# First attention of a two-layer kernel: another order of steps, later weighing of masked steps, and part of the second squares on ScalarE

## The reference

```python
# 16 heads of d = 16; rotary and a layernorm per head on q and k
a = einsum('bhnd,bhmd->bhnm', q, k) ** 4
a = tril(a)
out = einsum('bhnm,bhmd->bhnd', a / sum(a, -1), v) @ w_out
```

## Time and profile before

| | |
|---|---|
| three runs | 1670.02, 1672.91, 1682.65 us, median 1672.91 |
| profiled execution | 1666.9 us, of which the span of the trace is 1665.2 us |
| TensorE clock granted, mean | 0.88 of 2.4 GHz |
| TensorE busy | 1369.2 us (82%) |
| VectorE, ScalarE, GpSimd busy | 1083.1, 830.2, 570.2 us (65%, 50%, 34%) |
| first attention, both batches' steps | from 74 to 201 us and from 270 to 434 us |

### The profile page before, as it was taken

How to read it: one execution, slowest core, us unless ns; L and a number is a source line. 1 busy time by engine, 2 the same in 40 slices (tenths; PEclk the granted TensorE clock), 3 DMA queues, 4 the chain that set the end, 5 groups by cost and what they waited for, 6 DMA issues and landing times.

```text
span 1665.2 us, 27032 instructions
## 1 busy us (share of the span) xinstructions
PE 1369.2 (82%) x10104; PEld 880.1 (53%) x10104; DVE 1083.1 (65%) x2291; ACT 830.2 (50%) x1208; POOL 570.2 (34%) x674
## 2 busy tenths in 40 slices
PE   6377755686689999799999899889999886999982
PEld 4233443342468877444444555444554353799971
DVE  7678896866553354867777566667767545455676
ACT  2466625665343343236666355566657531366660
POOL 7477344547201103110111001001110476666660
PEclk8599985987789999759999899989989877999996
DMA  2690000002211100000000000000001355577875
GB/s 88 212 353 35 1 1 1 1 1 86 72 43 64 39 17 27 16 1 1 2 2 1 1 1 1 1 1 1 2 1 64 141 197 197 166 213 211 259 260 205
DMA packets 69078, 124.36 MB, mean 75 GB/s; under 512 B 7319, under 2 KB 55127, under 8 KB 67929
## 3 DMA queue, kind: packets, MB, share of 16 engines
q1 hardware_dynamic: 56664, 85.92, 16.1%
q0 software_dynamic: 12288, 36.72, 5.9%
HBM read 60.22 MB, written 62.39 MB: 74 GB/s over the span
## 4 chain that ended last, share of the span: by engine, by line
PE 56%; DVE 23%; POOL 8%; ACT 7%; issue 4%; DMA 1%; POOLq 0%; SPq 0%; DVEq 0%; ACTq 0%
PE psum L2283 10%; PE psum L2156 9%; PE psum L2256 6%; PE psum L2466 6%; DVE probs L2837 5%; PE psum L2373 4%; PE psum L2216 4%; DVE neg_max L2819 4%; PE psum L2489 3%; PE psum L2233 3%; PE psum L2394 3%; POOL many_x L3430 3%; PE psum L337 2%; POOL probs L3368 2%; ACT probs L2579 2%
## 5 line engine op out<-in xcount | busy, mean ns | idle before, releaser
L2579 ACT ACTIVATE probs<-psum 128x1024 f32<-128x1024 f32 (+1 forms) x480 | 437.4, 945 | 269.4 <-PE psum L2270 140.6
L2819 DVE TENSOR_REDUCE neg_max<-psum 128x1 f32<-128x512 f32 (+3 forms) x768 | 380.0, 551 | 132.5 <-PE psum L2233 118.4
L2256 PE MATMUL psum<-qt,kt 32*128 32x512 f32 (+6 forms) x1152 | 242.8, 454 | 31.0 <-ACT probs L2579 10.3
L2283 PE MATMUL psum<-probs,v 128*32 128x256 f32 (+3 forms) x2048 | 187.2, 453 | 58.4 <-POOL probs L3368 42.8
L2837 DVE TENSOR_TENSOR probs<-probs 128x1024 f32<-128x1024 f32 (+1 forms) x152 | 199.9, 1372 | 45.6 <-ACT probs L2579 45.2
L2216 PE MATMUL psum<-kt,qt 32*128 32x512 f32 (+3 forms) x768 | 205.2, 458 | 19.9 <-DVE neg_max L2819 18.5
L2256 PEld LDWEIGHTS psum<-qt,kt 32*128 32x128 f32 (+1 forms) x1152 | 108.9, 199 | 192.3 <-issue 98.4
L342 POOL TENSOR_SCALAR q_rows<-neg_max 128x16 fp32r<-128x16 f32 x32 | 7.1, 221 | 539.0 <-DVE neg_max L2827 358.8
L3437 POOL DMA_INDIRECT results<-sp_y,sp_row x128 | 124.8, 975 | 64.2 <-ACT sp_y L2634 37.6
L2216 PEld LDWEIGHTS psum<-kt,qt 32*128 32x128 f32 x768 | 96.0, 197 | 46.9 <-DVE neg_max L2819 39.1
L2156 PE MATMUL psum<-ident,q_rows 128*128 128x128 f32 x384 | 67.8, 320 | 57.8 <-ACT k_rows L2508 51.1
(11 more groups left out here) (327 smaller groups left out, 2602.1 us busy)
## 6 DMA issues: line engine op xcount, KB each, us to landing
many_x<-blank SPq DMA_DIRECT2D x2, 10240.0 KB, 50.9
sp_xs<-many_x SPq DMA_DIRECT2D x64, 320.0 KB, 3.7
sp_w<-in_sparse SPq DMA_DIRECT2D x8, 1280.0 KB, 10.2
x_turned<-results SPq DMA_DIRECT2D x8, 768.0 KB, 6.4
sp_back<-results SPq DMA_DIRECT2D x8, 768.0 KB, 9.2
sorted_x<-blank SPq DMA_DIRECT2D x2, 1152.0 KB, 6.5
sorted_y<-y SPq DMA_DIRECT2D x18, 128.0 KB, 1.7
rows<-in_x SPq DMA_DIRECT2D x4, 512.0 KB, 7.0
```

The lines of the kernel that those rows point to most:

```text
L2256: inst = pe.matmul(psum[:, base - early:base + QCH - q0], A.kt[rows, k_slot, key * P:(key + 1) * P], A.qt[rows, q_slot, c * QCH + q0 - ear ...
L2283: inst = pe.matmul(psum[32 * h:32 * h + 32, bank + q0:bank + q1], A.v_of(b)[:, key, col:col + 32], A.probs[:, slot, h, at:at + q1 - q0], s ...
L2579: act.activation(dst, view, ACT.Exp if A.softmax else ACT.Square).then_inc(exped.by(A.layer, b, quad, c, step, h0), 1)
L2819: inst = dve.tensor_reduce(A.neg_max[:, g % 2, 0 if last else 1, tile, h0 + i:h0 + i + 1], bank[:, at * P:(at + cols) * P], X_AXIS, ALU.ma ...
```

## The change

1. The steps of a quad run in the order of `MIXED_STEPS`, those of a batch's first quad in that of `FIRST_STEPS`.
2. A masked step is weighed after three further steps in place of two; unmasked ones after two as before. Which weighing opens and closes a bank is counted (`first`, `closes`) in place of taken from the step's number.
3. The second square of three halves, (1,1) h0=2, (1,2) h0=2 and (1,3) h0=0, is done by ScalarE right behind its first; GpSimd squares none.
4. The second half's cuts and turns of quad 0's groups move from before the quad into it, at places 0 to 2.
5. The next quad's cuts and turns stand at `CUT_PLACES`: cuts of the first group at 2.5 to 4 and its turn at 6 in a first quad, at 0 to 2.5 and 5 otherwise; of the second group at 4.5 to 6.2 and 9, or 4 to 6 and 8. Before: 0 to 2.4 and 3.75, 3.5 to 5.9 and 7.25.
6. Normalizing of the quad before stands at 3 (before 2.5); in the last quad chunk 0 is normalized at 8, turned at 9 and projected at 10, behind the last step (before 5.5, 7, 8.5).

```diff
+FIRST_STEPS = ((0, 0), (0, 1), (0, 2), (1, 0), (1, 4), (1, 1), (1, 5), (1, 2), (1, 6), (1, 3))
+RAISED_ON_ACT = ((1, 1, 2), (1, 2, 2), (1, 3, 0))
+MIXED_STEPS = ((0, 0), (1, 0), (0, 1), (0, 2), (1, 1), (1, 4), (1, 5), (1, 2), (1, 6), (1, 3))
+CUT_PLACES = (((2.5, 3, 3.5, 4, 6), (4.5, 5, 6.1, 6.2, 9)), ((0, 1, 2, 2.5, 5), (4, 4.5, 5.5, 6, 8)))
...
-                    def weigh_due():
-                        while due and len(due) >= WEIGHTS_AHEAD + (A.softmax and due[0][2] == 0):
-                            weigh()
+                    def weigh_due(n):
+                        for entry in [e for e in due if n - e[5] >= WEIGHTS_AHEAD + (e[2] >= 4 * e[1])]:
+                            weigh(entry)
...
-                            on_pool = c == 1 and step == 3 and h0 == 0
-                            if poly:
-                                done = mark(pool_raised if on_pool else raised, L, b, quad, c, step, h0)
+                            on_act = (c, step, h0) in RAISED_ON_ACT
+                            if on_act:
+                                done = mark(exped, L, b, quad, c, step, h0, "raised")
+                            elif poly:
+                                done = mark(raised, L, b, quad, c, step, h0)
...
-                        due.append((quad, c, step, p_slot, tuple(ready)))
-                        if poly and len(due) > WEIGHTS_AHEAD:
-                            weigh()
+                        n = next(steps_done)
+                        due.append((quad, c, step, p_slot, tuple(ready), n))
+                        weigh_due(n)
...
-                    else:
-                        for g in (0, 1):
-                            cut(g, HALF, TILES, hurry=True)
-                            turn(g, HALF, TILES)
...
-                            between.append((2.5, lambda q=quad - 1: normalize(q)))
+                            between.append((3, lambda q=quad - 1: normalize(q)))
+                        else:
+                            for g in (0, 1):
+                                between.append((g, lambda g=g: cut(g, HALF, TILES, hurry=True)))
+                                between.append((1 + g, lambda g=g: turn(g, HALF, TILES)))
...
-                            between.append((5.5, lambda q=quad: half_done.append(normalize(q, 0, HALF))))
-                            between.append((7, lambda: turn_out(0, half_done[0])))
-                            between.append((8.5, lambda: project_out(0)))
+                            between.append((8, lambda q=quad: half_done.append(normalize(q, 0, HALF))))
+                            between.append((9, lambda: turn_out(0, half_done[0])))
+                            between.append((10, lambda: project_out(0)))
...
# ScalarE
             def scores(A, b, quad, c, step, h0, p_slot, p_free, slot, qk_done, on_act, **_):
...
                 act.activation(dst, view, ACT.Exp if A.softmax else ACT.Square
                                ).then_inc(exped.by(A.layer, b, quad, c, step, h0), 1)
+                if on_act:
+                    q.wait_ge(exped, A.layer, b, quad, c, step, h0)
+                    act.activation(dst, dst, ACT.Square
+                                   ).then_inc(exped.by(A.layer, b, quad, c, step, h0, "raised"), 1)
...
# GpSimd
-            def scores(A, b, quad, c, step, h0, p_slot, slot, on_pool, **_):
-                if A.softmax or not on_pool:
-                    return
-                view, dst = scored_view(A, c, step, h0, p_slot, slot)
-                q.wait_ge(exped, A.layer, b, quad, c, step, h0)
-                pool.tensor_tensor(dst, dst, dst, ALU.mult).then_inc(pool_raised.by(A.layer, b, quad, c, step, h0), 1)
-                q.wait_ge(pool_raised, A.layer, b, quad, c, step, h0)
```

More of the change, by code:

```diff
@@ L731, in turn_max, with weigh @@
                            q_free=q_free, before=before)
[L733 to L738, removed]
+                    due, o_turn, chunk_weighed, steps_done = [], {}, {}, count()
+                    def weigh(entry):
+                        quad, c, step, slot, ready, _ = entry
+                        due.remove(entry)
+                        n = chunk_weighed.setdefault((quad, c), 0)
+                        chunk_weighed[quad, c] = n + 1
+                        first, closes, oc, oc_free = n == 0, n == len(key_steps(c)) - 1, None, ()
+                        bank_free = o_free[c] if first else ()
                         done = mark(weighed, L, b, quad, c, step, None)
                         probs_ring.give(slot, done)
-                        closes, oc, oc_free = step == len(key_steps(c)) - 1, None, ()
                         if closes:
@@ L910, in plan_attention @@
                         between.sort(key=lambda p: p[0])
-                        for n, (c, step) in enumerate((c, step) for c in range(SEQ // QCH) for step in range(len(key_steps(c)))):
+                        for n, (c, step) in enumerate(MIXED_STEPS if quad else FIRST_STEPS):
                             half_steps = weights(quad, c, step, beside[2 * n:2 * n + 2])
@@ L918, in plan_attention @@
                             what()
-                    while due:
-                        weigh()
+                    for entry in tuple(due):
+                        weigh(entry)
                     before_next = fence()
@@ L1095, in weigh @@
                     do("weigh", A=A, b=b, quad=quad, c=c, step=step, part=part, slot=slot, waits=(*ready, *bank_free),
-                       closes=closes, oc=oc, oc_free=oc_free)
+                       first=step == 0 and part == 0, closes=closes, oc=oc, oc_free=oc_free)
                 def weigh_due(half):
@@ L2272, in scores, with weigh @@
                     inst.then_inc(scored.by(A.layer, b, quad, c, step, h0), 1)
-            def weigh(A, b, quad, c, step, part, slot, waits, **_):
+            def weigh(A, b, quad, c, step, part, slot, waits, first, closes, **_):
                 bank = A.out_bank(c)
-                steps = key_steps(c)
                 for e in waits:
                     q.wait_ge(*e)
-                whole = [(key, first_query(c, key), QCH, at) for key, at in steps[step][0]]
+                whole = [(key, first_query(c, key), QCH, at) for key, at in key_steps(c)[step][0]]
                 for key, q0, q1, at in whole if part is None else weigh_parts(c, step)[part]:
@@ L2283, in weigh @@
                         inst = pe.matmul(psum[32 * h:32 * h + 32, bank + q0:bank + q1], A.v_of(b)[:, key, col:col + 32],
-                                         A.probs[:, slot, h, at:at + q1 - q0], start=step == 0 and not part,
-                                         stop=step == len(steps) - 1 and part != 0, skip_group_check=part is not None)
+                                         A.probs[:, slot, h, at:at + q1 - q0], start=first, stop=bool(closes),
+                                         skip_group_check=part is not None)
                 inst.then_inc(weighed.by(A.layer, b, quad, c, step, part), 1)
@@ L2572, in turn_max, with scores @@
                      ).then_inc(act_copied.by("max", b, g, half), 1)
-            def scores(A, b, quad, c, step, h0, p_slot, p_free, slot, qk_done, **_):
+            def scores(A, b, quad, c, step, h0, p_slot, p_free, slot, qk_done, on_act, **_):
                 view, dst = scored_view(A, c, step, h0, p_slot, slot)
@@ L2828, in cut_max, with scores @@
                                       ).then_inc(max_known.by(b, g, "both"), 1)
-            def scores(A, b, quad, c, step, h0, p_slot, slot, on_pool, before, maxima, **_):
+            def scores(A, b, quad, c, step, h0, p_slot, slot, on_act, before, maxima, **_):
                 if maxima:
                     max_unit(A, before, maxima)
-                if A.softmax or on_pool:
+                if A.softmax or on_act:
                     return
```

24 lines of the change are left out of this document (11 added, 13 removed).

## The result

Ten runs each gave a median of 1661.59 us (1652.53 to 1669.81) after and 1670.91 us before; the ratio is 0.994, with a 95% interval of 0.9913 to 0.9967, so 9 to 10 us less in place of 33.5. The profiled execution took 1661.7 us.

The account below looks back on a forecast made before the run. The prediction held the first attention bound by order and waits, VectorE nearest its limit; -14.5 us for batch 0 and -19 for batch 1 make -33.5, from 1672.9 to 1639 us, range 1617 to 1662.

Parts of the forecast that it names:

- What bounds the kernel: First attention: bound by order and waits, VectorE nearest its limit; weighing waits 42.8 us for masks, masks 73.8 for squares.
- rival (d): TensorE's turns wait for the second group's k rows on GpSimd: slower, up to +17.5 us, 1690; chance 0.06.
- The squares: Second squares per quad: VectorE 2.4 to 3.0 us less, GpSimd one square less, ScalarE 3.15 us more, in idle time.
- rival (b): VectorE and GpSimd never overlap, so quads 0 to 2 stay at 31.1 us or more: -24 us, 1649; chance 0.20.
- Mixed steps and later masks: Batch 0, quads 1 to 3: new order and a third step of room cover mask waits; -3, -4, -4.5 us.
- The start of a batch: Quad 0 of each batch: first square some 5.5 us sooner; -3 us in batch 0, -2.5 in batch 1.
- The last quads: Quad 3, without cuts: -4.5 us in batch 0, -8 in batch 1 with bounds -3 and -15.
- The sum: First attention, all quads: -14.5 us in batch 0 and -19 in batch 1, -33.5 together, nothing hiding it.
- (a): ScalarE becomes the bound, its added squares holding up PSUM release: only -8.5 us, 1664; chance 0.09.
- (e): The new order gains nothing, only half of 19 us of squares counts: -10 us, 1663; chance 0.06.

Follow-up runs that it names:

- run 9: Changed kernel with GpSimd's cuts ahead of the masks, normalizing at 5 and the second group's q cuts at 4: ratio 0.9817 to the kernel before, 1638.11 us.
- run 11: The kernel of run 9 with masked steps weighed after two further steps instead of three: ratio 0.988 to the kernel before.
- run 2: Changed kernel with only the cuts' places moved, ahead of the masks in GpSimd's queue: ratio 0.9869 to the kernel before.
- run 3: Changed kernel with the second half's cuts and turns back before quad 0: ratio 0.9925 to the kernel before.
- runs 1 and 10: All second squares on VectorE, against the changed kernel and against that of run 9: ratios 0.9986 and 0.9958 to the kernel before.

## Why the prediction was wrong

**What bounds the kernel.** Right as far as it went: masks behind squares. It read GpSimd as an engine with 25.5 of 32.0 us of busy time, and asked what else stands in its queue only in rival (d). Its borders of quads 1 to 3 are wrong, as told above: in batch 0, quad 0 took 38.4 us and not 34.0, quad 2 32.5 and not 34.0, and the last quads took 30.9 and 51.1 and not 33.7 and 54.0.

**The squares.** Right in size: ScalarE's square out of SBUF takes 1.06 us (1.05 was taken), 24 of them; ScalarE rose to 25.15 us in quad 1 (25.0), VectorE fell to 21.2 (5.5 us less, for 3.0), its large squares from 1.49 to 1.39 us on the average, all 136 together to 1.29 (1.30). The sum of VectorE's and GpSimd's undisturbed times was no bound, though: with it quads with cuts had a floor of 31.1 us for rival (b), and run 9 does all the work of one, 17 squares, 8 masks and 16 cut instructions, in 28.8 us (the next, in 27.8, starts five cut instructions fewer). The Trainium skill's exclusive lock ("SBUF — State Buffer", SBUF: two separate sides) fits the direction: in the changed kernel's trace all 44 of GpSimd's cut copies that run beside no square take 0.40 to 0.42 us, and 23 of the 28 beside one take 1.25 or more. But summing whole instructions as if each held it from end to end is refuted here. Beside each other, from 112.42 us on, squares and copies both start 1.34 us apart; alone they start 1.13 and 0.49 apart, 1.62 together.

**Mixed steps and later masks: the step that failed.** "Forecast 29, from 32.0: -3. Quad 2, the same work in 34.0: 30, -4." Measured 32.8 and 33.7 us, +0.8 and +1.1. The term counted the mask waits that go (they did go, 42.8 to 1.9, and run 11 shows that the step of room does it) and nothing that comes. What came is rival (d) in kind, a wait of the turns for GpSimd's rows, with its own sign, waits of over 3 us for k_rows; but it came at the first group's turns too (12 of the 28.8 us), where (d) named the second's alone. It was given a chance of 0.06 and weighed only for its slower end; but the waits needn't reach 5.6 us per quad to matter. They came to 28.8 us in all, 4.3 at the longest, and taking them away (run 2) gives back 9.8 us of the stage. The reason given against it, "two whole steps lie between", counted steps of TensorE, where GpSimd's queue had a mask between the place and the cut, and that mask waits for VectorE. With cuts and normalizing moved (run 9) the stage is 32.5 us shorter than before, near to the 33.5 forecast, though for another kernel than the one forecast.

**The start of a batch.** Forecast -3 and -2.5, measured +0.8 and +0.5. The first square did come early, at 69.99 us against 75.40 on VectorE. By run 3 the start itself takes 4.8 and 3.6 us off the first quads, and the rest of the change adds 5.6 and 4.1. Most of that, by run 2, is the next groups' cuts, "so that they no longer stand between the first masks": they now stand behind all three. GpSimd makes them from 80.97 on, and TensorE's turns wait 2.6, 1.2 and 3.2 us for them; with the cuts ahead 3.1 and 4.7 us come back. The clock granted to TensorE in the first quad also fell, from 0.79 to 0.69 of 2.4 GHz (0.71 with the start undone); the runs don't part this from the waits.

**The last quads.** Batch 0's takes 29.2 us, the very number forecast, but by luck: it had taken 30.9 before, not 33.7, and gained 1.6 in place of 4.5, although VectorE's busy time fell from 29.1 to 24.3 us; what holds it now isn't shown. Batch 1's went to 41.2 us from 51.1, -9.9 for a forecast of -8 within its bounds: the 6.66 us wait behind the indirect DMAs is gone, and there were no cuts to hold up. Quad 1 of batch 1 gained 2.3 for 5; its turns wait 5.7 us for GpSimd's rows. Quad 2 gained nothing for 3.5, and there no turn waits for GpSimd: the weighing's waits for squares and masks went (5.2 us), and in their place TensorE waits for the router's work on VectorE, 3.3 us at one place.

**The sum.** By quads +0.8 + 0.8 + 1.1 - 1.6 = +1.1 for batch 0 (forecast -14.5) and +0.5 - 2.3 + 0.3 - 9.9 = -11.4 for batch 1 (forecast -19). The two quads without cuts gained 11.5 us for 12.5 forecast; the six with cuts were forecast to gain 21 us together and lost 1.2. The measured 1661.6 us lies just inside the range of 1617 to 1662, and that is luck. It is near the times of (a) and (e) as well, 1664 and 1663, but runs 1 and 10 speak against (a), as the stage grows by 9.8 and 17.6 us without ScalarE's squares, and runs 2 and 9 against (e), as places in the queues alone free the gain.

## What to carry to other kernels

When a change gives one product of an engine more room, list what stands behind it in that engine's queue: work that depends on nothing late belongs ahead of the instruction that waits, not behind it. A wait that goes to nearly nothing while the time hardly moves has a successor; look for it on the same engine first, under another line. When parts of two traces are compared, cut both at the same instruction, and check that it is the one you mean: here borders that were 3 to 4 us off made two first quads look 5.2 and 3.5 us slower that are slower by 0.8 and 0.5. And two halves of a change can each measure as nothing and still be worth having together, so undo them one at a time from the changed kernel as well as adding them to the old one.

## What the runs showed that I had not expected

ScalarE's squares alone, in the old order, gained nothing (1.0027), although VectorE's busy time for large squares fell from 172.7 to 137.5 us and its idle time ahead of them rose from 45.0 to 88.2: the freed time became waiting. Removing all masks shortened the stage by only 22.6 us from the changed kernel, and run 9 reaches 22.2 of these with the masks in. And the same kernel, the one before, took 1668 us beside one set of runs and 1784 and 1778 beside the others; the changed kernel's stage was 294.8 us in one trace and 295.8 in a trace from the slower sets, so the difference is not in the first attention, and a single time from another chip would have drowned every effect told of here.
